# Cross-attention and a routed FFN on one core: ranks' places written tile by tile, and the last columns of W1 and of W2 in one tile of 128

## What is computed

```
x = x + xattn(layernorm(x), ctx, ctx, mask)          # 16 heads, float32
y = layernorm(x)
scores = y @ w_router;  idx = top_k(scores, 128)     # 128 of 512 tokens
x_sel = y[idx]
x_attn = causal_attention(rmsnorm(x_sel, g1))        # W_qkv, W_out
h2 = rmsnorm(x_sel + x_attn, g2)
x_ff = (silu(h2 @ W1.T) * (h2 @ W2.T)) @ W3.T        # W1, W2: (682, 256)
y[idx] = x_sel + x_attn + x_ff
x = x + y
```

## Time and profile before

| | us |
|---|---|
| median of three runs | 889.56 |
| lowest, highest | 888.82, 891.79 |
| the profiled execution | 880.62 |
| its span, first to last instruction | 878.9 |
| PE busy in the span | 852.3 |
| ACT busy | 570.7 |
| DVE busy | 312.4 |
| POOL busy | 122.7 |

### The profile page before, as it was taken

One profiled execution on the slowest core, in us unless ns is written; L12 is line 12 of the kernel. 1 busy time (PEld: TensorE's weight loads), 2 busy tenths in 40 slices (PEclk: granted clock), 3 DMA queues, 4 the chain that ended last, 5 costly groups with the idle time before them and its releaser, 6 DMA issues. The chain is left out here.

```text
span 878.9 us, 28281 instructions
## 1 busy us (share of the span) xinstructions
PE 852.3 (97%) x11797; PEld 297.4 (34%) x11802; DVE 312.4 (36%) x915; ACT 570.7 (65%) x648; POOL 122.7 (14%) x174
## 2 busy tenths in 40 slices
PE   7999999999999999999999999999999999999875
PEld 2322232334323433334323333233323342234343
DVE  3122245421552326421453216522274213322442
ACT  3567667676677767676677766777676766776310
POOL 4000102110120101111121101201021101200111
PEclk9999999999999999999999999999999999999999
DMA  5060101120011200211011200112002100010000
GB/s 186 14 234 3 64 17 33 54 76 11 3 37 50 80 8 27 61 32 50 8 39 50 80 8 2 37 50 80 7 5 60 32 3 7 14 49 3 7 25 11
DMA packets 27579, 35.58 MB, mean 40 GB/s; under 512 B 2083, under 2 KB 24142, under 8 KB 27448
## 3 DMA queue, kind: packets, MB, share of 16 engines
q1 hardware_dynamic: 24952, 31.73, 11.3%
q0 software_dynamic: 2496, 1.98, 1.4%
HBM read 27.53 MB, written 8.93 MB: 41 GB/s over the span
## 5 line engine op out<-in xcount | busy, mean ns | idle before, releaser
L524 ACT ACTIVATE probs<-pair_bank 128x1024 f32<-128x1024 f32 x512 | 496.4, 1021 | 222.9 <-ACTq L523 221.7
L494 PE MATMUL pair_bank<-q_sb,k_sb 32*64 32x512 f32 x4096 | 291.2, 612 | 0.4 <-PEq L492 0.3
L513 PE MATMUL o_bank<-probs,va 128*32 128x512 f32 x2048 | 274.7, 604 | 3.0 <-issue 1.5
L513 PEld LDWEIGHTS o_bank<-probs,va 128*32 128x32 f32 x2048 | 41.7, 108 | 208.2 <-issue 113.8
L494 PEld LDWEIGHTS pair_bank<-q_sb,k_sb 32*64 32x64 f32 x4096 | 62.3, 129 | 134.8 <-issue 133.5
L271 PE MATMUL m_bank<-wv_sb,ctx_in 128*32 128x256 f32 x1024 | 62.2, 380 | 0.0
L271 PE MATMUL m_bank<-ctx_in,wk_sb 128*32 128x512 f32 x480 | 61.0, 592 | 0.0
L649 DVE TENSOR_SCALAR va<-m_bank,valid 128x256 f32<-128x256 f32 x64 | 28.1, 479 | 82.8 <-DVEq L646 82.7
L605 DVE STREAM_TRANSPOSE o_blk<-o_bank 128x512 f32<-128x512 f32 x32 | 22.9, 717 | 96.4 <-DVEq L604 96.4
L271 PEld LDWEIGHTS m_bank<-wv_sb,ctx_in 128*32 128x32 f32 x1024 | 33.5, 110 | 35.9 <-issue 21.3
L271 PEld LDWEIGHTS m_bank<-hid_t,w 128*32 128x32 f32 x1392 | 39.4, 110 | 17.2 <-issue 16.3
(11 more groups left out here) (175 smaller groups left out, 627.3 us busy)
## 6 DMA issues: line engine op xcount, KB each, us to landing
ctx_in<-in_ctxT SPq DMA_DIRECT2D x7, 1024.0 KB, 4.9
x_in<-in_x SPq DMA_DIRECT2D x8, 512.0 KB, 3.9
x<-in_x SPq DMA_DIRECT2D x8, 512.0 KB, 4.3
mask_in<-in_mask SPq DMA_DIRECT2D x8, 512.0 KB, 3.9
out_dram<-base SPq DMA_DIRECT2D x8, 512.0 KB, 5.6
ctx_in<-in_ctxT SPq DMA_DIRECT2D x2, 512.0 KB, 6.9
mask_row<-in_mask SPq DMA_DIRECT2D x8, 128.0 KB, 3.9
x_tok<-in_order SPq DMA_DIRECT2D x7, 128.5 KB, 2.0
```

The costliest lines, as they stand in the source:

```text
L494: last = nc.tensor.matmul(pair_bank[pairs[r // 2]][j:j + 64, r % 2], key_tile(b, s, r)[:, j:j + 64], query_tile(b, s, r), start=True, stop ...
L513: last = nc.tensor.matmul(o_bank[32 * r:32 * r + 32], va[b % 2][:, t, HV * h:HV * h + 32], probs[s % 2][:, r], start=(t == 0), stop=(t == ...
L524: nc.scalar.activation(probs[s % 2][:, 2 * e:2 * e + 2, :], pair_bank[p][:], ACT.Exp, scale=HD ** -0.5).then_inc(s_free[p], 1)
```

## The change

- `put(t)` is called at the end of its own stage `order<t>`, behind a drain. Before, it was called one stage later, and the last two together at the end of `order3`. `select` and `select_tile` keep the old scheme.
- The last tile of `w1` holds W1's last 42 columns in its columns 0 to 41, as before, and W2's last 42 columns in its columns 64 to 105. `w2` has five tiles. The third product of `u1` then gives W1's rest on partitions 0 to 41 and W2's rest on partitions 64 to 105 of the bank, and `w1` (the stage) has two products left of three.
- On DVE stage `u1` gets a second instruction, which copies half of W2's rest from partitions 64 to 105 of the bank to partitions 0 to 41 of `w_rest`; the bank is released behind it. Stage `w1` gets an instruction that multiplies `w_rest` with the rest's `silu2`, ahead of its wait for PE, and its old instruction is 256 columns wide in place of 384.
- At the start POOL zeroes the last tile of `gate` in place of `w2`'s columns, and SP issues 11 DMAs in place of 10: W2's load is cut in two.

```
+REST = DFF - (FT - 1) * P
+W2_REST = 64
@@ pe_ffn, u and w
-                for f in range(3):
+                for f in range(2 if stage == "w1" else 3):
@@ dve_ffn, order and rank
-                if t > 0:
+                if note is put:
+                    dve.drain()
+                    put(t)
+                elif t > 0:
                     note(t - 1)
-                if t == QT - 1:
+                if t == QT - 1 and note is not put:
                     dve.drain()
                     note(t)
@@ dve_ffn, u0 and u1
-                nc.vector.scalar_tensor_tensor(out=silu2[r][:], in0=half_tanh[r][:], scalar=1.0, in1=bank[i][:, 0:3 * P],
-                                               op0=ALU.add, op1=ALU.mult).then_inc(bank_free[i], 1)
+                last = nc.vector.scalar_tensor_tensor(out=silu2[r][:], in0=half_tanh[r][:], scalar=1.0, in1=bank[i][:, 0:3 * P],
+                                                      op0=ALU.add, op1=ALU.mult)
+                if r == 1:
+
+                    last = nc.vector.tensor_scalar(w_rest[:], bank[i][W2_REST:W2_REST + REST, 2 * P:3 * P], 0.5, None, ALU.mult)
+                last.then_inc(bank_free[i], 1)
@@ dve_ffn, w0 and w1
                 r = int(stage[1])
+                if r == 1:
+                    nc.vector.tensor_tensor(gate[0:REST, FT - 1], w_rest[:], silu2[r][0:REST, 2 * P:3 * P], ALU.mult)
                 dve.wait_ge(done["w"], 1)
                 dve.sem_inc(done["w"], -1)
-                nc.vector.scalar_tensor_tensor(out=gate[:, 3 * r:3 * r + 3].rearrange("p f k -> p (f k)"), in0=bank[i][:, 0:3 * P],
-                                               scalar=0.5, in1=silu2[r][:], op0=ALU.mult, op1=ALU.mult
+                n = 3 - r
+                nc.vector.scalar_tensor_tensor(out=gate[:, 3 * r:3 * r + n].rearrange("p f k -> p (f k)"),
+                                               in0=bank[i][:, 0:n * P], scalar=0.5, in1=silu2[r][:, 0:n * P],
+                                               op0=ALU.mult, op1=ALU.mult
                                                ).then_inc(bank_free[i], 1)
@@ loads
-                sp.dma_start(w2[:, :, 0:DFF], io["w2T"].rearrange("(c p) n -> p c n", p=P)).then_inc(w_in["ffn_w"], 16)
+                w2_in = io["w2T"].rearrange("(c p) n -> p c n", p=P)
+                whole = (FT - 1) * P
+                sp.dma_start(w2[:], w2_in[:, :, 0:whole]).then_inc(w_in["ffn_w"], 16)
+                sp.dma_start(w1[:, :, whole + W2_REST:whole + W2_REST + REST], w2_in[:, :, whole:DFF]).then_inc(w_in["ffn_w"], 16)
@@ zeros
-                nc.gpsimd.memset(w2[:, :, DFF:], 0.0)
+                nc.gpsimd.memset(gate[:, FT - 1], 0.0)
```

More of the change, by code:

```diff
@@ L124, in program @@
         wout = sb("wout", [P, KC, D])
-        w1, w2 = (sb(n, [P, KC, FT * P]) for n in ("w1", "w2"))
+        w1, w2 = sb("w1", [P, KC, FT * P]), sb("w2", [P, KC, (FT - 1) * P])
         w3 = sb("w3", [P, FT, D])
@@ L188, in program @@
         silu2 = [sb(f"silu2{r}", [P, 3 * P]) for r in range(2)]
+        w_rest = sb("w_rest", [REST, P])
         gate = sb("gate", [P, FT, P])
@@ L1284, in _ @@
                 general_sync(sp)
-            N_FFN_W = 10
+            N_FFN_W = 11
             @block.gpsimd
```

## The result

The changed kernel takes 877.61 us (median of 4 runs, 876.77 to 879.77) beside 889.19 us of the kernel before (4 runs, 888.12 to 891.79): ratio 0.9869, 95% interval 0.9841 to 0.9897. The prediction had put this profile at 878.5; that it came near is luck, as the experiments will show.

What follows compares the result with a forecast made beforehand. PE, busy 97%, was taken to bound the pipeline, the chain the last block. Terms -3.08 + 0.70 + 0.30 = -2.1 us; from the 889.56 us median that gave 887.5 us, range 886.0 to 889.6.

Steps and rivals of the forecast that it cites:

- the sum: Whole kernel: -2.1 us (-3.1 to -1.3), 878.5 us profiled; carrying over 8.9 us to the median gave 887.5 us.
- Places written earlier: `order` stages: x_tok lands some 1.3 us earlier, which buys nothing; drains and `put`s cost nothing; zero.
- Rival D: Earlier scatter gives PE something after all: up to 1.3 us more in element 7, 886.2 us; chance 0.05.
- The cover: Element 7: `hid` ready at 766.25 us, PE's `hidT` due only at 768.38, so earlier x_tok gains nothing.
- Matmuls removed: Stage `w1`: one of three products goes, 0.44 us under each of seven elements, 3.08 us gained.
- the bank held longer: Stage `u1`: second DVE instruction frees `m_bank` 0.35 us later, costing PE 0.10 us, seven times: +0.70 us (0 to 1.33).
- Rival A: Second DVE instruction overlaps the first, so no stall in `w1`: -2.9 us, 886.7 us; chance 0.30.
- B: PE's products did not limit the `w1` step, or the gain is lost again: +0 to +0.3, about 889.8 us; chance 0.08.
- C: The instruction across partitions is long and `m_bank` stalls PE in each `w1`: at 1.1 us, +4.0, 893.5 us; chance 0.05.
- The last block: Last FFN block: the gate of `w0` waits behind the new DVE instruction, delaying `down`: +0.30 us (0 to 0.44).
- The start: Kernel start: one more DMA and a swapped memset cost nothing, since element 1 first needs the weights; zero.
- The prediction's own sign: Stated test: the prediction is wrong if some step other than that of `w1` has changed its length.

Runs made afterwards that it cites:

- the places alone: Kernel before with only the `put` change, places written tile by tile: 882.34 us, ratio 0.9929 on chip 14; 885.74 us, 0.9950 on chip 15.
- third scatter earlier: Kernel before with `put(1)` moved ahead of `order2`'s compares, so POOL's third indirect DMA starts earlier: 878.84 us, ratio 0.9879.
- shared tile only: Changed kernel with the places written as before, leaving only the shared tile of W1 and W2: 884.39 us, ratio 0.9945.
- better kernel: Kernel before plus the shared W1/W2 tile and `put(1)` ahead of `order2`'s compares: 876.21 us, ratio 0.9848 on chip 15; 876.79 us, 0.9970 on chip 2.
- third later: Kernel before with a useless DVE memset ahead of the second place, so the later indirect DMAs start later: 888.78 us, ratio 0.9993.
- both held: Kernel before with the third and fourth indirect DMA held until DVE passed the queries' stage: 888.31 us, ratio 0.9987 on chip 15; 891.45 us, 1.0126 on chip 10.

## Why the prediction was wrong

Two steps failed together: the sum was put on a base that its trace doesn't show, and the term of the places, which acts on just that part of the base, was put at zero.

**The sum ended in the wrong base.** "The median of the runs shown lies 8.9 above that execution; I carry the difference over." By their step 11 and their times, the profiled execution is of the kind of chip at 880 and the median of the kind at 889 (neither chip was noted), and the 8.9 us were no constant: they were, nearly all, six stalls of 1.5 us in step 11, which that trace doesn't contain, and which this change shortens. No row of the trace could give their cause; that a profile lies 1% below the lowest of three runs that agree within 0.3% could have given the doubt, and with it a range that reaches lower.

**"Places written earlier ... Zero."** Right for the chip that the trace came from: x_tok earlier buys nothing, `put` and drain cost nothing. Wrong for the chip of the median. Writing `place` in its own stage sends the fourth scatter 0.6 to 1.1 us earlier against PE's signal (t4 from +0.18 to -0.46 or -0.95), and so DVE starts 0.7 to 1.3 us earlier. The six steps went from 31.53 to 24.86 us, a gain of 6.67 for a term of zero (6.8 with the places alone; 6.9 by the medians). The wait for POOL's transfers was looked at only as data (when does x_tok land), not as something that disturbs a hand-over between other engines. Rival D had the place, with another mechanism (x_tok) and a fifth of the size. The cover that the prediction read for `hid` in element 7, 766.25 against 768.38, was mostly chance too: PE stood for 1.54 us in the middle of the values ahead of that `hidT`, with nothing named that it waited for:

```profile
767.40 1.05 PE L513 MATMUL o_bank<-probs,va 128*32 128x512 f32 x4 [1.54 <-issue]
```

With the third scatter earlier, `hidT` there followed the end of `hid` by 0.31.

**Matmuls removed and the bank held longer.** Right. -0.44 + 0.10 was to give 3.0 us; it is 2.97. The instruction lasts 0.293 us (forecast 0.30), its gap is +0.02 (forecast +0.05), so the bank is free 0.31 later and PE loses 0.06 in place of 0.10: 7 x 0.38 = 2.66 us gained, forecast 2.38. Rival A's overlap (a gap of -0.08) did not happen. The Trainium skill ("VectorE: DVE Perf Modes", section "Two Vector instructions with no wait between them") says that an instruction whose input starts in another group of 32 partitions than the last one read from that memory is held until the earlier ones have finished; the trace agrees, with a gap of 0.02 us. Rivals B and C are out by the same rows.

**The last block.** Right where it was forecast: +0.30 us, 2.03 against 1.73, the gate being what is late. From the last step's scores to the end, 61.3 us before and 60.7 in the changed kernel, it can't be seen.

**The start.** No change that shows: first scores at 17.98 us, 18.14 and 18.27 in two executions of before.

**The whole.** Between the profiles of before on chip 14 (span 886.6) and of the changed kernel (875.8), 10.8 us: 6.67 from step 11, 2.66 from step 28, less 0.30 in the last block, and 1.8 in a few single steps, the start and element 7. Between the two profiles taken on chip 14 it is 9.4 us, 6.2 of them from step 11. The largest of these is step 12 of element 0, 4.06 us before, 4.06 with places only, 3.78 with the shared tile only, but 2.96, 3.24, 3.51 and 4.06 in four executions of the changed kernel: it varies with nothing changed, and is no effect of the change that can be shown. The prediction's own sign, "I am wrong if some step other than that of `w1` has changed its length", did come, in step 11. Where no stall is seen, the corrected sum is -2.66 + 0.30 = -2.4 us, inside the measured 1.5 to 4.5, as is the forecast's -2.1.

**Still open.** Why two kinds of chips exist and what in the chip is held; the runs show only when, and not without exceptions. That it is PE's signal is the simplest reading, not a shown one: DVE and ACT start late while PE goes on, and a hold on the readers, for instance on the supply of their instructions, was not tested against it. Element 3 with the shared tile only and element 3 of the better kernel (t3 -0.99, t4 +0.28 in both) should have been held and were not. On the chips with the stall these two are also the only elements in which DVE pauses for 0.43 to 0.44 us, with nothing named that it waits for, ahead of `order3`'s first compare; what that has to do with it was not followed. In two elements (third later, element 6; changed on chip 15, element 3) DVE starts 2.28 and 2.24 behind the third scatter, and so it does, by 2.18 to 2.23, in step 12 of five elements with both held; that is neither 1.55 nor 2.95. And ACT's signal, due 1.32 behind the fourth scatter where the third goes earlier, is held in 2 elements of 11 only. That the scatters cause the stall is shown; the numbers of 1.5 us a scatter describe most elements and explain none.

## What to carry to other kernels

When the profiled execution and the median of the runs differ by more than the runs among themselves, find out what differs before building a sum on either: profile the kernel again beside the runs, and compare step lengths. On a chip like the three at 889, an indirect DMA issued by POOL was not free for engines that have nothing to do with it: see which hand-overs from PE fall within 1.6 us behind its start (3 us where two follow each other), and move it by some tenths of a microsecond before anything larger is tried. Here, delaying it with a wait moved the stall and made its data late.

## What the runs showed of the hardware

- On three chips of five, a signal from PE that is due 0.6 to 1.35 us behind the start of a POOL indirect DMA reaches DVE, in nearly all elements, only 1.51 to 1.61 us behind that start (up to 1.63 on chip 15, 1.64 to 1.71 where it had first fallen behind the start of the DMA before). With two DMAs 1.28 to 1.43 us apart, DVE's start is 2.92 to 3.03 us behind the first of them in both cases. ACT is held too: with the kernel before on chip 14 its exponential starts at s + 1.93 in place of 1.24, 0.07 behind DVE, though in other placings it mostly is not. On the two other chips the same placings hold nothing. A signal due 0.33 behind a start was not held.
- POOL's row for this DMA ends 0.97 us behind its start, 0.58 before DVE starts. The row's end is thus not the end of its effects. The Trainium skill ("Perfetto Trace Analysis", section "DMA Instruction — SWDGE (GPSIMD)") says that the profile's end is when the last DSP has made its descriptors, not when the data have moved; the 0.58 agrees with it but does not prove what the engine does in that time.
- The same program on one core runs at 880 us on two chips and at 889 on three, 1% apart, and these stalls account for nearly all of it: 8.9 us in the profiles, and the third-earlier kernel, which has none, runs at 878.8 on a chip of the 889 kind. Each chip was seen in one group of runs only.
